# The causal mask of attention's first pass in constant contraction rows of Q and K, not in a matmul of its own

## What is computed

```python
q = jnp.einsum('bsd,hdk->bhsk', embeddings, Wq) + bq[None, :, None, :]
k = jnp.einsum('bsd,hdk->bhsk', embeddings, Wk) + bk[None, :, None, :]
v = jnp.einsum('bsd,hdk->bhsk', embeddings, Wv) + bv[None, :, None, :]
scores = jnp.einsum('bhqk,bhsk->bhqs', q, k) / jnp.sqrt(jnp.float32(dk))
causal_mask = jnp.triu(jnp.ones((s, s), dtype=bool), k=1)
scores = jnp.where(causal_mask, jnp.float32(-1000000000.0), scores)
weights = jax.nn.softmax(scores, axis=-1)
ctx = jnp.einsum('bhqs,bhsk->bhqk', weights, v)
concat = ctx.transpose(0, 2, 1, 3).reshape(b, s, d)
return concat @ Wo + bo
```

## Time and profile before

| | us |
|---|---|
| median of 3 runs | 1685.39 |
| lowest, highest | 1681.05, 1686.82 |
| span of the profiled execution | 1684.0 |
| busy: PE, DVE, ACT, POOL | 1346.8, 1232.3, 895.3, 916.5 |
| matmuls | 7325 |
| L1984, maxima of the first pass, x624 | 368.6 |
| L2252, first-pass matmuls, x768 | 233.8 |
| L2255, mask matmuls, x512 | 102.7 |
| L2271, scores, x768 | 180.9 |

### The profile page before, as it was taken

The page is one execution under the profiler, slowest core; times in us unless marked ns, Lnnn a source line. Parts: engine busy times, 40 slices in busy tenths (PEclk is TensorE's granted clock), DMA queues, the critical chain, the costliest instruction groups (busy, mean ns, idle before and its releaser), DMA issues. The chain is left out here.

```text
span 1684.0 us, 25407 instructions
## 1 busy us (share of the span) xinstructions
PE 1346.8 (80%) x7325; PEld 726.0 (43%) x7325; DVE 1232.3 (73%) x2340; ACT 895.3 (53%) x1660; POOL 916.5 (54%) x746
## 2 busy tenths in 40 slices
PE   6848888888888989999536899999899998822756
PEld 2313333333333378999523344443343343211743
DVE  6999999999998643252576988889889888260324
ACT  5746666566665645566324166655555565701423
POOL 1479889999897037352642012113463455674773
PEclk9879999999999979999868899999999999955877
DMA  1029100000000045787506212111221113311317
GB/s 56 0 68 343 38 0 0 0 0 0 0 0 0 1 113 165 200 231 203 140 21 211 60 31 57 34 31 31 75 62 35 39 43 77 79 18 45 102 52 251
DMA packets 121420, 122.69 MB, mean 73 GB/s; under 512 B 29778, under 2 KB 96575, under 8 KB 118904
## 3 DMA queue, kind: packets, MB, share of 16 engines
q1 hardware_dynamic: 99404, 97.47, 20.7%
q0 software_dynamic: 10240, 15.79, 3.3%
q10 hardware_dynamic: 11660, 8.01, 1.6%
HBM read 76.68 MB, written 50.52 MB: 76 GB/s over the span
## 5 line engine op out<-in xcount | busy, mean ns | idle before, releaser
L1962 ACT ACTIVATE t_PT<-t_ps_s 128x1024 f32<-128x1024 f32 (+3 forms) x384 | 294.2, 811 | 229.5 <-PE t_ps_s L2271 228.4
L1984 DVE TENSOR_REDUCE t_negm<-t_ps 128x1 f32<-128x512 f32 (+4 forms) x624 | 368.6, 640 | 59.7 <-PE t_ps L2252 30.9
L464 POOL TENSOR_TENSOR s_HC<-s_H,X 128x1024 f32<-128x1024 f32 x128 | 307.1, 2417 | 40.0 <-DVE s_H L585 31.0
L629 PE MATMUL ps_y<-s_HC,ident 128*128 128x512 f32 x512 | 268.4, 649 | 20.9 <-POOL s_HC L464 19.4
L2252 PE MATMUL t_ps<-heads 128*128 128x512 bf16 (+3 forms) x768 | 233.8, 341 | 34.8 <-DVE t_negm L1984 21.6
L1896 POOL TENSOR_SCALAR_AFFINE_SELECT t_PT<-t_PT 128x512 f32<-128x512 f32 x128 | 84.4, 659 | 310.7 <-ACT t_PT L1962 310.4
L2271 PE MATMUL t_ps_s<-heads 128*128 128x512 bf16 (+3 forms) x768 | 180.9, 329 | 3.8 <-ACT t_PT L1962 2.1
L2286 PE MATMUL t_ps_c<-t_PT,t_VG 128*32 128x512 f32 (+3 forms) x1536 | 164.3, 501 | 1.1 <-ACT t_CT L1924 0.6
L525 ACT ACTIVATE s_dA<-m_DT,s_A 128x512 f32 (+1 forms) x192 | 127.5, 712 | 59.1 <-DVE s_H L585 58.2
L2252 PEld LDWEIGHTS t_ps<-heads 128*128 128x128 bf16 x768 | 73.3, 99 | 198.3 <-DVE t_negm L1984 142.4
L629 PEld LDWEIGHTS ps_y<-s_HC,ident 128*128 128x128 f32 x512 | 97.0, 201 | 124.1 <-issue 68.7
(11 more groups left out here) (337 smaller groups left out, 2368.5 us busy)
## 6 DMA issues: line engine op xcount, KB each, us to landing
f_w<-in_W_dram SPq DMA_DIRECT2D x93, 256.0 KB, 5.3
heads<-token_expert_rows SPq DMA_DIRECT2D x8, 1024.0 KB, 12.7
token_expert_rows<-X SPq DMA_DIRECT2D x42, 192.0 KB, 2.7
heads<-q_parts SPq DMA_DIRECT2D x42, 192.0 KB
heads<-k_parts SPq DMA_DIRECT2D x14, 576.0 KB
expert_rows<-X SPq DMA_DIRECT2D x27, 192.0 KB, 2.4
f_XS<-expert_rows SPq DMA_DIRECT2D x19, 256.0 KB
expert_rows_out<-f_YB ACTq DMA_DIRECT2D x19, 256.0 KB
```

The source lines that it names most:

```text
L464: nc.gpsimd.tensor_tensor(HC[:, g % RING], H[:, g % RING], row_wide(C_sb[:, g % RING, :], 2), ALU.mult).then_inc(s_hc, 2)
L629: nc.tensor.matmul(ps_y[c][:], ident[:], HC[:, g % RING, c, :], start=g == 0, stop=g == N - 1, skip_group_check=True).then_inc(s_y, 1)
L1962: nc.scalar.activation(PT[:, n % RP, 2 * p:2 * p + 2, 0:wd], src, ACT.Exp, scale=DK ** -0.5).then_inc(s_exp, 1)
L1984: nc.vector.tensor_reduce(out, ps_1[use % BANKS1][:, 0:h * width].rearrange("p (h k) -> p h k", h=h), AX.X, ALU.max, negate=True).then_inc ...
```

## The change

The mask goes into rows 96 to 127 (`MASK_AT = 96`) of Q[g] and K[g]. These 32 rows hold step functions, so that the 32 products add up, for every key behind the query, to at least 2^24 in size and negative, and for the others to at most 2^-10. Row 96 + r belongs to queries and keys 4r to 4r + 3 of every tile of 128: Q has powers of two there for its four queries and zero elsewhere, K has powers of two for its four keys, and a large negative constant for all later ones. A matmul over all 128 rows so gives scores with the mask, one over rows 0 to 95 gives them without.

In `item` a diagonal piece is now two matmuls side by side, the columns ahead of the diagonal tile over 96 rows and the last 128 columns over 128 rows; the identity matmul is gone. Where a piece is the diagonal tile alone (query tiles 0 and 4) there is one matmul. Everything else in both passes contracts over rows 0 to 95.

GpSimd builds the steps in float32 in `steps` with nine selections, converts them to the rows of Q[0] and K[0] and copies them over all 32 tiles (four heads, eight tiles). It fills only rows 0 to 95 with constants, Q[0] and K[0] ahead of the steps, the other six behind. SP copies the 32 rows from Q[0] to Q[1..3] and from K[0] to K[1..3], six transfers of 256 KB, behind its last store. PE waits for the rows ahead of the first item of each of groups 0 to 3 (`s_mr`).

```diff
@@ sync, in attn_project
+            sp.wait_ge(s_mr[0], 2)
+            for g in range(1, NG):
+                for own, first in ((Q[g], Q[0]), (K[g], K[0])):
+                    sp.dma_start(own[MASK_AT:P].rearrange("r j t -> r (j t)"), first[MASK_AT:P].rearrange("r j t -> r (j t)")).then_inc(s_mr[g], 16)
             sp.wait_ge(s_d[1], 16 * 2 * PARTS)
             sp.wait_ge(s_d[2], 16 * 2 * PARTS * 2)
@@ gpsimd
-            nc.gpsimd.memset(maskf[:], 0.0).then_inc(s_z, 1)
             nc.gpsimd.memset(zero[:], 0.0).then_inc(s_z, 1)
-            pool.wait_ge(s_z, 2)
-            nc.gpsimd.affine_select(out=maskf[:], in_=maskf[:], compare_op=ALU.is_ge, fill=NEG, base=0,
-                                    pattern=[[-1, P]], channel_multiplier=1).then_inc(s_z, 1)
+            nc.gpsimd.memset(steps[:], 0.0).then_inc(s_st, 1)
             for g in range(NG):
-                nc.gpsimd.memset(Q[g][:].rearrange("p j t -> p (j t)").bitcast(F32), 0.0).then_inc(s_q, 1)
-                nc.gpsimd.memset(K[g][:].rearrange("p j t -> p (j t)").bitcast(F32), TWO_ONES).then_inc(s_q, 1)
-            pool.wait_ge(s_z, 3)
-            nc.gpsimd.tensor_copy(mask[:], maskf[:]).then_inc(keep["s_mb"], 1)
-            nc.gpsimd.tensor_copy(identb[:], keep["ident"][:]).then_inc(keep["s_mb"], 1)
+                nc.gpsimd.memset(Q[g][0:MASK_AT].rearrange("p j t -> p (j t)").bitcast(F32), 0.0).then_inc(s_q, 1)
+                nc.gpsimd.memset(K[g][0:MASK_AT].rearrange("p j t -> p (j t)").bitcast(F32), TWO_ONES).then_inc(s_q, 1)
+                if g:
+                    continue
+                pool.wait_ge(s_st, 1)
+                later = steps[:, 1]
+                nc.gpsimd.affine_select(out=later, in_=later, compare_op=ALU.is_ge, fill=-2.0 ** (K_LOW + BASE * STEP), base=-MASK_AT,
+                                        pattern=[[-1, P // STEP], [0, STEP]], channel_multiplier=1).then_inc(s_st, 1)
+                pool.wait_ge(s_st, 2)
+                for d in range(STEP):
+                    for x, fill in ((0, 2.0 ** (Q_TOP - BASE * d)), (1, -2.0 ** (K_LOW + BASE * d))):
+                        own = steps[:, x, :, d]
+                        nc.gpsimd.affine_select(out=own, in_=own, compare_op=ALU.not_equal, fill=fill, base=MASK_AT,
+                                                pattern=[[1, P // STEP]], channel_multiplier=-1).then_inc(s_st, 1)
+                pool.wait_ge(s_st, 2 + 2 * STEP)
+                for x, rows in enumerate((Q[0], K[0])):
+                    tiles = rows[MASK_AT:P].rearrange("p j (t n) -> p (j t) n", n=P)
+                    nc.gpsimd.tensor_copy(tiles, row_wide(steps[MASK_AT:P, x].rearrange("p r d -> p (r d)"), GH * QT)).then_inc(s_mr[0], 1)
@@ tensor, in item
+                    if b == 0:
+                        pe.wait_ge(s_mr[g], 32 if g else 2)
                 pe.wait_ge(s_mx, use + 1)
+                plain = width - P if diagonal else width
                 for u in range(h):
-                    mm = nc.tensor.matmul(out[:, u * width:(u + 1) * width], Q[g][:, j + u, qt * P:(qt + 1) * P],
-                                          K[g][:, j + u, c * CH:c * CH + width], start=True, stop=not diagonal, skip_group_check=True)
+                    if plain:
+                        mm = nc.tensor.matmul(out[:, u * width:u * width + plain], Q[g][0:MASK_AT, j + u, qt * P:(qt + 1) * P],
+                                              K[g][0:MASK_AT, j + u, c * CH:c * CH + plain], start=True, stop=True, skip_group_check=True)
                     if diagonal:
-                        mm = nc.tensor.matmul(out[:, (u + 1) * width - P:(u + 1) * width], identb[:], mask[:], start=False, stop=True,
-                                              skip_group_check=True)
+                        mm = nc.tensor.matmul(out[:, u * width + plain:(u + 1) * width], Q[g][:, j + u, qt * P:(qt + 1) * P],
+                                              K[g][:, j + u, qt * P:(qt + 1) * P], start=True, stop=True, skip_group_check=True)
@@ tensor, in scores
-                    mm = nc.tensor.matmul(ps_s[p][:, h * CH:h * CH + wd], K[g][:, 2 * p + h, kt * P:(kt + 1) * P],
-                                          Q[g][:, 2 * p + h, c * CH + r * P:(c + 1) * CH], start=True, stop=True)
+                    mm = nc.tensor.matmul(ps_s[p][:, h * CH:h * CH + wd], K[g][0:MASK_AT, 2 * p + h, kt * P:(kt + 1) * P],
+                                          Q[g][0:MASK_AT, 2 * p + h, c * CH + r * P:(c + 1) * CH], start=True, stop=True)
```

More of the change, by code:

```diff
@@ L1473 @@
 VW = 32
-NEG = -1e30
+STEP = 4
+MASK_AT = P - P // STEP
+BASE = 34
+Q_TOP, K_LOW = 50, -60
 BLOCKS = [(c, kt, max(kt - c * PER, 0)) for c in range(2) for kt in range((c + 1) * PER)]
@@ L1518, in attn_project @@
     X2, Vt, Q, K = keep["X2"], keep["Vt"], keep["Q"], keep["K"]
-    maskf, mask, identb = keep["maskf"], keep["mask"], keep["identb"]
     with ExitStack() as ctx:
@@ L1525, in attn_project @@
         zero = sb("zero", [P, 2 * CH], BF16)
+        steps = sb("steps", [P, 2, P // STEP, STEP])
         parts = sb("parts", [P, 2, 2, PARTS, SEQ], BF16)
@@ L1542, in _ @@
         def _(sp):
-            sp.wait_ge(s_z, 3)
+            sp.wait_ge(s_z, 1)
             sp.dma_start(dram["zeros"].rearrange("r (a n) -> (r a) n", a=GH), zero[0:PARTS * GH, :]).then_inc(s_zd, 16)
@@ L1741, in attend_and_route @@
         mp = sb("mp", [GH * QT, 2, PARTS, P], BF16)
-        mask, identb, s_mb = keep["mask"], keep["identb"], keep["s_mb"]
+        s_mr = keep["s_mr"]
         w = sb("w", [P, P])
@@ L2238, in _ @@
             pe.sem_inc(s_pv, RP)
-            pe.wait_ge(s_mb, 2)
             def item(gi, n, use):
@@ L2395, in attention @@
         sb = lambda n, s, d=F32: ctx.enter_context(nc.sbuf_tensor("c_" + n, s, d))
-        own = dict(keep, maskf=sb("maskf", [P, P]), mask=sb("mask", [P, P], BF16), identb=sb("identb", [P, P], BF16),
-                   s_d=[ctx.enter_context(nc.semaphore(f"parts_stored{k}")) for k in range(3)],
-                   s_mb=ctx.enter_context(nc.semaphore("mask")), Vt=sb("Vt", [P, NT, P]), Q=[QK[:, 2 * g] for g in range(NG)], K=[QK[:, 2 * g + 1] for g in range(NG)],
+        own = dict(keep, s_d=[ctx.enter_context(nc.semaphore(f"parts_stored{k}")) for k in range(3)],
+                   s_mr=[ctx.enter_context(nc.semaphore(f"mask_rows{g}")) for g in range(NG)], Vt=sb("Vt", [P, NT, P]), Q=[QK[:, 2 * g] for g in range(NG)], K=[QK[:, 2 * g + 1] for g in range(NG)],
                    s_ld=[ctx.enter_context(nc.semaphore(f"heads_loaded{g}")) for g in range(NG)])
```

3 lines of the change are left out of this document (2 added, 1 removed).

## The result

The changed kernel takes 1692.56 us (median; 1686.02 to 1705.02), the kernel before 1685.45 in the runs beside it: a ratio of 1.0056, with a 95% interval of 1.0033 to 1.008. It is slower by 0.6%, where 1668 was forecast. The profiled execution spans 1689.7 us against 1684.0; the first line is the page's head.

A forecast was written before the change was run, and what follows sets the result against it. TensorE was taken to bound plain attention windows, VectorE the first two groups. Savings of 0.3 + 13.9 + 4.3 = 18.5 us, less 1.0, gave 17.5: 1685.4 - 17.5 = 1668 us, range 1660 to 1681 (85%).

The forecast's parts named there:

- Step (1): TensorE, per group: 32 mask matmuls at 0.056 us save 1.79 us, splitting costs 0.05, net 1.74 us.
- Step (2), the nine full windows: Attention windows with PE busy 98 to 100%: each gives 1.54 us, 13.9 us saved in all.
- the stretch of the first twelve items: Start of a group, where VectorE also makes max parts: three banks absorb most of 0.5 us, 0.2 us taken off.
- Step (2), the routing windows: Five attention windows with routing mixed in (two g = 2, three g = 1): half counted, 0.87 us each, 4.3 us saved.
- Step (3): SP ahead of attention: six transfers take 2.2 to 3.8 us to issue; the projection's block ends later, +0.4 us.
- My rival at 1.70 each: Six SP issues at 1.70 us take 10.2 us, ending at 921.1 against 912.9; 9.8 us saved, 1676; chance 5%.
- Step (4): GpSimd in the projection: selections and two conversions of 3.6 us each are hidden; VectorE slows slightly, +0.5 us.
- Step (5): Attention's first items: the wait on mask rows is over before, and using 96 rows costs nothing.
- the slow load: Loading 96 rows of weights makes a step some 0.11 us, 1.7 us a group: 1686, the same; chance 8%.
- the drain: Switching between 96 and 128 rows costs up to 0.08 us, 54 switches a group: slower, 1722; chance 7%.
- VectorE takes over: Only 16 of 32 masks count in the nine windows, routing windows give nothing: 7.4 us saved, 1678; chance 15%.
- Six transfers stall: DMA engines run full when SP issues the six mask-row transfers: 10.2 us of issues, 9.8 us saved, 1676; chance 5%.

The follow-up runs named there:

- the run with eleven out: Kernel before with GpSimd's bias addition moved to the g = 3 groups, 11 of a group's 32 mask matmuls left out: plain window 29.26 us.
- the run with the short chain: All mended, with the last two of VectorE's four operations splitting the turned maxima left out from the third group on: plain window 27.95 us.
- narrower maxima: All mended, with the maxima of items 8 to 11 of each group taken over the middle 256 columns only: plain windows 28.28 us.
- the run with 96 rows alone: Kernel before, masks as they were, plain matmuls and scores over rows 0 to 95: 1689.70 us beside 1689.59 for the kernel before.
- all mended: Changed kernel with mask-row copies issued in attention's block, bias addition in g = 3 groups, each conversion cut in four: 1672.51 us, 0.993 of the kernel before.

## Why the prediction was wrong, point by point

**Step (1), the price of a mask: right.** 0.056 us a step, and the 21 masks that the run with eleven out left in are worth 21 x 0.056 = 1.18 us, which with 0.11 for the eleven gives 1.29; without masks the window fell by 1.17, and by 1.08 with the pieces split. The price of splitting, 0.05 us, was too low by the busy times (up to 0.4).

**Step (2), the nine full windows: the right kind, too large.** 8.1 us instead of 13.9. The term that was mis-sized is the 0.2 us taken off for the stretch of the first twelve items: in a regular plain window it is 0.66. The six plain windows gave 6.9 us of 9.2 forecast, with the 0.7 of luck. I had read the right rows, but as VectorE's total work, of which three banks absorb most; it is a chain of latencies, and the masks that lie beside it are covered. The three g = 0 windows gave 0.39 each, a quarter, and make the larger part of this miss (3.4 of 5.8 us). Without masks and without constant rows they still give only 0.49, so it is not the change's own cost. The same chain is 0.33 of it, shown by the run with the short chain; VectorE's total work is not, since narrower maxima changed nothing. The rest stays open: TensorE's two further waits for maxima stand there and were not tested.

**Step (2), the routing windows: wrong, and the largest miss.** 4.3 us saved was forecast, 6.5 lost was measured. The other three routing windows (two with g = 2, and the first with g = 1, hit in both kernels) gave 1.4. The two later g = 1 windows met a collision that the kernel before had in one window of three. The row that told of it was in the trace: of the norm's 32 tiles one took 2.39 us against a median of 0.34, and 2.4 is the length of GpSimd's addition. I took the first g = 1 window's length, 41.18 against 37.21 and 36.40, for the price of routing and never asked why one of three alike was 4 us longer.

**Step (3), six issues: mis-sized.** 2.4 us in all was taken, from issues of 0.37 to 0.63 us; it was 7.0. My rival at 1.70 each had the mechanism and was given 5%; the measured size is 1.17 each. The prediction even named that the DMA engines run full there and still took the row from a quiet place. Cost: 6.4 us.

**Step (4), the conversions: the durations right, the cover wrong.** 3.6 us each was close (7.94 for two). That they were hidden was argued from buffers and waits alone; L1623, with its two on-chip inputs, stands still beside them. Without the issues the block is 1.3 us longer than before (39.6 against 38.3), and dividing the conversions gives 1.9 back, 0.6 more than it was longer, which stays unexplained. The 0.1 us that I took for VectorE beside GpSimd came from fills, which only write: beside them a pair takes 1.42 us, without them 1.35.

The Trainium skill, page "GPSIMD Engine Reference", section "Specifications", says that GpSimd shares its interfaces to on-chip memory with VectorE, with contention for VectorE instructions in a two-port mode or with two inputs there. The traces agree: L1623 (two such inputs) and L2083 stood, L1628 and the maxima (PSUM) did not. L2083 has one tensor as input, from and to on-chip memory in float32; that it ran in a two-port mode is not shown by any row. The price is in the traces: the VectorE instruction is done only once GpSimd's is over, and took 2.4 to 3.9 us. This rule spoke against the change, and I did not weigh it.

**Step (5): right.** Nobody waited for the mask rows, and 96 rows cost 0.1 us in a plain window. The rivals of the slow load and of the drain are refuted by the steps and by the run with 96 rows alone. The Trainium skill, page "TensorEngine Tiling (Array Packing)", section "Tiling Modes", has no mode of 96 rows; that they run in the one of 128, and no mode changes, agrees with 0.002 us a switch.

**The rivals.** "VectorE takes over" predicted that early masks are worth nothing and the routing windows give nothing; the first is nearly so (0.11 us for eleven), though not for its reason. "Six transfers stall" was right in kind. None had the collision, and none that ended slower was the true one.

Adding up what was missed: 5.8 us in the nine windows, 10.9 in the routing windows, 6.7 in the block (7.7 for 1.0), less 0.2 elsewhere, are 23.2 us, and the forecast of 17.5 saved was off by exactly that from the 5.7 lost.

## What to carry to other kernels

Where one engine's instruction has a maximum far above its median, find what ran beside it before costing any change: a collision that hits one of three like windows can hit the others as soon as something moves; here 0.4 us was enough. By these runs, work put on GpSimd is not hidden if it reads tensors while VectorE works from on-chip memory to on-chip memory, as L1623 and L2083 do; where that can't be avoided, cut it in short pieces, as the conversions here (1.0 to 1.5 us each), which lost 2.9 us instead of 5.1. And by these runs a matmul is worth its step only where no chain of another engine's latencies runs beside it: look for a distance between two events that stays the same when the work between them changes.

## What the hardware showed unexpectedly

- A VectorE operation beside a tensor instruction of GpSimd can stand until that is over: one of 0.34 us became 2.4 to 3.0 beside an addition of 2.4, and a pair of 1.42 us became 4.69 beside a conversion of 3.9. Maxima from PSUM ran at their usual 0.6 to 0.7 us, and fills did next to nothing.
- Issuing a 256 KB transfer from SP took 1.02 to 1.17 us on average while the DMA engines moved some 290 to 330 GB/s, against 0.37 for the loads of heads at a quieter time.
- A wait of 2.64 us on TensorE was followed by 4.2 us at a mean granted clock of 0.70 and 4 us at 0.88, which cost another 1.8 us, an estimate from these two means. With the addition moved and the wait gone (all mended), the same stretch had 1.00.
- Alternating 96 and 128 contraction rows costs about 0.002 us a switch in the plain windows, and 0.005 at most in the others.
- Eleven mask matmuls with 0.62 us of steps were worth 0.11 us, and six of them lay beside a chain of four short VectorE operations and a maximum, which set the distance between two events at 1.80 us with and without them.
